# Attention units: order of decay exponentials and scores, place of the normalisation, and gate and finish steps on GpSimd

## What is computed

```python
qkvgr = einsum('btc,oc->bto', layernorm(x), W)         # q, k, v (16 heads of 8) and 16 gates
log_G = cumsum(log_sigmoid(gates), axis=time)          # per head
Z = 2*log(abs(q @ k.T) + 1e-7) + log(scale) + log_G[t] - log_G[s]     # causal
P = exp(Z - rowmax);  y = (P @ v) / sum(P);  x = x + y
```

## Time and profile before

| | |
|---|---|
| three executions | 1281.03, 1281.9, 1283.69 us, median 1281.9 |
| the profiled execution | 1283.27 us |
| its span, first to last instruction | 1281.4 us |
| attention, units of all batches | from 36 to 462 us of the span |
| busy in the span | PE 884.1, PEld 610.8, DVE 769.8, ACT 531.4, POOL 502.0 us |
| granted TensorE clock, mean | 0.816 of full |

### The profile page before, as it was taken

How to read it: one execution, slowest core, us unless ns; L and a number is a source line. 1 busy time by engine, 2 the same in 40 slices (tenths; PEclk the granted TensorE clock), 3 DMA queues, 4 the chain that set the end, 5 groups by cost and what they waited for, 6 DMA issues and landing times. The chain is left out here.

```text
span 1281.4 us, 25926 instructions
## 1 busy us (share of the span) xinstructions
PE 884.1 (69%) x9215; PEld 610.8 (48%) x9215; DVE 769.8 (60%) x1623; ACT 531.4 (41%) x1192; POOL 502.0 (39%) x545
## 2 busy tenths in 40 slices
PE   4778778786877834079937599947776783407993
PEld 2445354453644521068823278616565572106882
DVE  6576685766766674012254079999999999401223
ACT  4557465565646621034514430025555540104441
POOL 3452434534345321714430000027777770172442
PEclk9978696887968867579978889977888887758997
DMA  6133140322404041167732930000002100016775
GB/s 188 48 115 103 38 140 14 128 71 70 137 5 140 2 166 45 54 164 197 206 101 102 254 74 1 1 0 1 0 0 65 33 17 17 11 54 166 203 198 160
DMA packets 134915, 111.75 MB, mean 87 GB/s; under 512 B 27248, under 2 KB 120368, under 8 KB 134384
## 3 DMA queue, kind: packets, MB, share of 16 engines
q1 hardware_dynamic: 129264, 99.66, 26.3%
q0 software_dynamic: 5120, 10.53, 2.4%
q10 hardware_dynamic: 432, 0.20, 0.1%
HBM read 64.80 MB, written 45.43 MB: 86 GB/s over the span
## 5 line engine op out<-in xcount | busy, mean ns | idle before, releaser
L624 DVE TENSOR_SCALAR a_mag<-a_pS 128x1024 int32<-128x1024 int32 (+1 forms) x192 | 176.7, 949 | 90.6 <-PE a_pS L831 90.6
L406 ACT ACTIVATE a_pw<-a_mag,a_eps_a 128x1024 f32<-128x1024 f32 (+1 forms) x192 | 173.4, 930 | 98.0 <-DVE a_mag L624 93.3
L299 POOL TENSOR_TENSOR a_pw<-a_pw,a_decay 128x256 f32<-128x256 f32 x128 | 97.2, 763 | 244.8 <-ACT a_pw L406 244.7
L1125 POOL DMA_INDIRECT ys_dram<-f_yo,f_who x96 | 91.9, 958 | 129.4 <-DVE f_yo L1325 112.7
L1313 DVE TENSOR_SCALAR f_ysT<-f_bY,f_b2s 128x256 f32<-128x256 f32 x48 | 23.2, 483 | 175.8 <-PE f_bY L1413 173.2
L831 PE MATMUL a_pS<-a_qf,a_kf 64*64 64x192 bf16 (+3 forms) x1536 | 115.6, 278 | 14.8 <-DVE a_mag L624 13.1
L1672 POOL TENSOR_TENSOR d_pb_p<-d_Q,d_s_sb 128x512 f32<-128x512 f32 x32 | 37.3, 1166 | 196.4 <-ACT d_s_sb L1772 196.4
L1168 ACT ACTIVATE f_hs<-f_bH,f_b1s 128x256 f32<-128x256 f32 x192 | 75.4, 475 | 66.5 <-PE f_bH L1403 66.5
L2145 PE MATMUL d_c<-d_pb_p,d_ident 128*128 128x256 f32 x256 | 73.5, 457 | 41.8 <-POOL d_pb_p L1678 41.8
L1117 POOL DMA_INDIRECT xs_dram<-f_xa,f_pos x64 | 61.6, 962 | 93.9 <-DVE f_pos L1298 75.0
L1403 PE MATMUL f_bH<-f_xsT,f_w1s 128*128 128x256 f32 x384 | 95.2, 392 | 0.0
(11 more groups left out here) (342 smaller groups left out, 1777.6 us busy)
## 6 DMA issues: line engine op xcount, KB each, us to landing
parts_scratch<-a_parts SPq DMA_DIRECT2D x32, 384.0 KB, 3.3
f_w1s<-in_L_ffn_w_dram SPq DMA_DIRECT2D x48, 256.0 KB
f_w2s<-in_L_ffn_w_dram SPq DMA_DIRECT2D x48, 256.0 KB
a_kf<-parts_scratch SPq DMA_DIRECT2D x16, 512.0 KB, 5.1
a_qf<-parts_scratch SPq DMA_DIRECT2D x16, 512.0 KB, 6.2
xs_dram<-blank SPq DMA_DIRECT2D x12, 516.0 KB, 5.3
f_xs<-xs_dram SPq DMA_DIRECT2D x48, 129.0 KB, 2.3
parts_scratch<-a_parts SPq DMA_DIRECT2D x16, 256.0 KB, 3.0
```

The lines of the kernel that those rows point to most:

```text
L299: pool.tensor_tensor(own, own, decay[:, k, m, hf:NP:2, :], ALU.mult)\
L406: act.activation(pw[:, n % 4, 0:N], mag[:, n % 3, 0:N], ACT.Square, bias=eps_a[:, 0:1])\
L624: dve.tensor_scalar(mag[:, n % 3, 0:2 * N].bitcast(I32).rearrange("p (l t) -> p l t", l=2), pS[:, 2 * (n % 2):2 * (n % 2) + 2, 0:N].bitcas ...
L1125: pool.indirect_dma_start(ys_dram[f][:, :], bass.IndirectOffsetOnAxis(ap=who[:, q, a:a + 1], axis=0), yo[:, q, a, :], None).then_inc(ys_ou ...
```

## The change

- The steps TURN, QK and VALUES come one step earlier (4, 6, 9), and the second half's finish too (FIN 18, 2). The value copies on ScalarE so move from step 14 to 13, `gate_logs` stays at 13.
- ScalarE: `decays` come first in their step, ahead of off_copy and square.
- TensorE: `scores(n + 2)` come first in their step.
- VectorE: `normalize` moves from step 20 to TURN + 1 = 5. The steps on the gates (`gate_low`, which were the second half of `gate_prep`, and `gate_log`) leave it for all batches but the first, and so do product and addition of the finish (L654, L659) for all halves but the very last.
- GpSimd takes them: `add_half` for the second half at step 4 and for the first half at step 20, `gate_low` at step 12 (three instructions, where VectorE had two) and `gate_log` at step 14, each behind that step's diagonal; add_half and gate_low are ahead of that step's `values_off` and `split_low`. `split_low` stays at steps 10 and 11.

```diff
-        TURN, QK, VALUES, SUMS, DECAY = 5, 7, 10, 15, 22
-        FIN = (18, 3)
+        TURN, QK, VALUES, SUMS, DECAY = 4, 6, 9, 15, 22
+        FIN = (18, 2)
@@ gpsimd @@
+            def gate_low(bb):
+                pool.wait_ge(s["gate_sb"], 4 * bb + 3)
+                pool.wait_ge(s["logg_done"], bb)
+                pool.tensor_scalar(g_low[:, :], gates[:, :], 0.0, None, ALU.min).then_inc(s["gate_sb"], 1)
+                pool.wait_ge(s["gate_sb"], 4 * bb + 4)
+                step(pool.tensor_tensor(g_abs[:, :], g_low[:, :], gates[:, :], ALU.subtract))
+                pool.tensor_tensor(g_abs[:, :], g_abs[:, :], g_low[:, :], ALU.add).then_inc(s["g_step"], 1)
+            def gate_log(bb):
+                pool.wait_ge(s["g_step"], 3 * bb + 3)
+                pool.wait_ge(s["cum_ps"], bb)
+                pool.tensor_tensor(logg[:, :], g_low[:, :], g_abs[:, :], ALU.subtract).then_inc(s["logg_done"], 1)
+            def add_half(b, k, hf):
+                step = 5 * (2 * b + hf)
+                pool.wait_ge(s["fin_step"], step + 3)
+                pool.tensor_tensor(y[:, :, :, :], acc[:, :, :, 0:HD],
+                                   rnorm[:, :, :].unsqueeze(3).broadcast_to([P, 16, 2, HD]), ALU.mult)\
+                    .then_inc(s["fin_step"], 1)
+                pool.wait_ge(s["fin_step"], step + 4)
+                xs = x[:, TT * b:TT * b + TT, :].rearrange("p i (a c) -> p (i a) c", c=32)[:, :, 16 * hf:16 * hf + 16]
+                pool.tensor_tensor(xs, xs, y[:, :, :, :].rearrange("p a x d -> p a (x d)"), ALU.add)\
+                    .then_inc(s["fin_step"], 1)
...
+                    if n == FIN[1] + 2 and not first:
+                        add_half(b - 1, 1 - k, 1)
+                    if n == FIN[0] + 2:
+                        add_half(b, k, 0)
                     if last:
                         continue
-                    if QK + 3 <= n < QK + 5:
-                        split_low(b + 1, n - QK - 3)
+                    if n == VALUES + 3:
+                        gate_low(b + 1)
+                    if n == VALUES + 5:
+                        gate_log(b + 1)
+                    if QK + 4 <= n < QK + 6:
+                        split_low(b + 1, n - QK - 4)
@@ scalar: batch @@
                 for n in range(NU):
+                    if not first:
+                        for m in decay_pair(n + NU - DECAY - 1):
+                            decays(b, k, m)
+                    if not last:
+                        for m in decay_pair(n - DECAY - 1):
+                            decays(b + 1, 1 - k, m)
                     if n == 1 and not first:
                         off_copy(b - 1, 1)
                     if n == HU + 1:
                         off_copy(b, 0)
                     square(b, n)
...
-                    if n == VALUES + 3:
+                    if n == VALUES + 4:
                         gate_logs(b + 1)
@@ vector: batch @@
                     if n == FIN[0] + 1:
-                        for part in (2, 3, 4):
-                            finish(b, k, 0, part)
+                        finish(b, k, 0, 2)
                     if n == FIN[1] + 1 and not first:
-                        for part in (2, 3, 4):
-                            finish(b - 1, 1 - k, 1, part)
+                        finish(b - 1, 1 - k, 1, 2)
...
-                    if n == 20 and b + 2 < B:
+                    if n == TURN + 1 and b + 2 < B:
                         normalize(b + 2)
...
-                    if n == VALUES + 3:
-                        gate_log(b + 1)
@@ tensor: batch @@
                 for n in range(NU):
+                    if n + 2 < NU:
+                        scores(b, k, n + 2)
+                    elif not last:
+                        scores(b + 1, 1 - k, n + 2 - NU)
                     if n == FIN[1] and not first:
                         turn_back(b - 1, 1)
...
-                    if n + 2 < NU:
-                        scores(b, k, n + 2)
-                    elif not last:
-                        scores(b + 1, 1 - k, n + 2 - NU)
```

More of the change, by code:

```diff
@@ L422, in batch @@
                     square(b, n)
-                    if not first:
-                        for m in decay_pair(n + NU - DECAY - 1):
-                            decays(b, k, m)
                     if last:
                         continue
-                    for m in decay_pair(n - DECAY - 1):
-                        decays(b + 1, 1 - k, m)
                     if n == TURN + 1:
@@ L556, in gate_prep @@
                 dve.wait_ge(s["v_ps"], bb + 1)
+                if bb:
+                    dve.wait_ge(s["g_step"], 3 * bb - 2)
                 for q, M in enumerate((M0, M1)):
@@ L678, in _ @@
             gate_prep(0)
+            gate_low(0)
             rstds(1, B, 6)
```

## The result

| | median of runs, us | lowest to highest | ratio to before, 95% interval |
|---|---|---|---|
| before | 1282.29 | 1281.03 to 1283.69 | |
| after | 1271.55 | 1268.58 to 1273.27 | 0.9914, 0.9892 to 0.9935 |

What follows compares the result with a forecast made beforehand. No engine is full in the attention; TensorE, busiest (some 43 of a batch's 54 us), waits most for ScalarE's decay exponentials, 31.1 us. Terms: -31.1 + 0 + 9.8 + 0.7 = -20.6 us, forecast 1262 us, range 1245 to 1276.

Steps and rivals of the forecast that it cites:

- The two waits at the boundary: Between batches, decay sums wait 1.66 us (the first) and 2.33 us for ScalarE's exponentials; both go, gain 31.1 us.
- The gate chain: Steps 13 to 14: gate_log on GpSimd behind diagonal(14) starts gate sums 1.4 us later: +9.8 us, bounds 6 to 13.
- Steps 2 to 11: Normalisation moves in at 1.0 to 2.3 us, finish work of 0.85 leaves; taken as 0, bounds -3 to +9 us.
- The turn-back's 6.4 us: Steps 16 to 21: TensorE's wait for the turn-back, 6.4 us over the seven-boundary stretch, claimed to stay.
- The last batch: End of the attention: add_half at step 20 delays diagonal(21) by 1.5 us, VectorE gains: +0.7 us, bounds 0 to 1.5.
- The two rivals on GpSimd: Released waits return on GpSimd's queue, steps 20 to 23 (1272, 12%), or its lock with VectorE at step 5 (1274, 11%).
- the second rival: Step 5: normalisation blocked by GpSimd instructions takes 3.0 us instead of 1.0; +12 us, 1274 us, 11%.
- I follow TensorE from step 22 (about 192) with the clock as it was: At the boundary, TensorE's steps costed at 1.2 GHz as before: scores 1.0, two decay sums 2.1, attend 0.4 to 0.7 us.
- low time in steps 15 to 21 is harmless: Argument against the slower rival: VectorE sets the pace in steps 15 to 21, so low clock there costs nothing.
- the slower rival: Longer idle before the gate sums (2.9 us, not 1.45) holds the low clock through steps 2 to 14: 1295 us, 5%.
- The clock rival: Boundary: without its two idle times TensorE gets 2.4 GHz earlier, 17 us more gained: 1245 us, 17%.
- the prediction's own signs: Attention in the profile after: a mean clock clearly under 0.8 would make the forecast wrong.

Runs made afterwards that it cites:

- e1: The kernel before with only ScalarE's decays moved to the head of their step: 1238.5 us, ratio 0.9665.
- e2: The kernel before with only the normalisation moved from step 20 to step TURN + 1: 1263.1 us, ratio 0.9853.
- e3: The changed kernel with gate_log on GpSimd at step 13 instead of 14, ahead of diagonal(14): 1257.9 us, ratio 0.9786.
- e12: The changed kernel with gate_log on GpSimd at step 13 and scores back in their old place: 1252.5 us, ratio 0.9770.
- e8: The changed kernel with scores back in their old place in TensorE's step: 1264.7 us, ratio 0.9839.
- e6: e1 plus the normalisation moved to step TURN + 1: 1240.0 us, ratio 0.9636.
- e7: e1 plus product and addition of each half's finish on GpSimd (add_half): 1243.8 us, ratio 0.9681.
- e11: e1 with the value copies on ScalarE moved to step 13, ahead of square(14): 1241.5 us, ratio 0.9694.
- e9: e1 with scores first in TensorE's step only in steps 22, 23, 0 and 1: 1261.5 us, ratio 0.9846.
- e10: e1 with scores first in TensorE's step only in steps 2 to 21: 1252.3 us, ratio 0.9696.
- e4: The changed kernel with the value copies on ScalarE back behind square(14), at step 14: 1259.5 us, ratio 0.9739.

## Why the prediction was right in its range, and off by half in its gain

- **The two waits at the boundary** (-31.1): right in cause and size. L812's waits went from 31.1 us to none, and the boundary stretch (scores(22) to scores(4) of the next batch) from 22.5 to 18.2 us, 29.1 us less over the seven. Right also that the first wait belonged to normalisation and order together: e1 and e2 each remove it.
- **The gate chain** (+9.8): right. The waits grew by 9.6 us, at 2.84 a batch against the 2.9 forecast, and taking the chain away gives 13.7 back (e3). But the steps behind them grew by 13.6 us, see below. The size of gate_low was short: 0.53 and twice 0.46 us instead of 0.4 each; its slack hid that.
- **Steps 2 to 11** (0, bounds -3 to +9): +2.7 us in steps 2 to 14, inside. The normalisation's four instructions took 1.9 us, within the 1.0 to 2.3 allowed for. The turn-back's 6.4 us, said to stay, went; the waits of scores for magnitudes took 5 of them.
- **The last batch** (+0.7): +1.1 us, from its scores(4) to the end of the attention.
- **The two rivals on GpSimd** did not come in: attends wait for GpSimd 7.8 us against 7.2, and the normalisation's four instructions take 1.9 us where the second rival has 3.0.
- **The step that failed** is "I follow TensorE from step 22 (about 192) with the clock as it was", which the sum does everywhere, together with "low time in steps 15 to 21 is harmless". The sum treated busy time as fixed; it rose by 13.8 us (338.0 to 351.9), which is more than the whole distance between 20.6 forecast and 11.8 found in the attention. Most of the rise, 9.0 us, is in steps 15 to 19. These were at a clock of 1.00 in four of the seven batches before, and are at 0.75 to 0.87 in all seven after, behind the 2.84 us wait. They last 12.6 to 13.1 us where the clock is 0.86 or 0.87 and 13.6 where it is 0.75; before, at 1.00, they lasted 10.8, and the longer wait alone would add 1.4. So the stretch grew by 13.6 us and not by 9.8. This is the mechanism of the slower rival at a small size, in the steps where the prediction ruled it out. Without the long wait these steps are at 1.00 again in five (e3) and seven (e12) of the seven batches; but of the busy time of the whole attention only 2.6 us come back in e3, and 6.9 from e8 to e12. So the wait brings the low clock to these steps, and what holds the total up is open.
- **The sum again, by stretches**: -29.1 + 13.6 + 2.7 + 1.1 gives the 11.8 found, to 0.1. The boundary was forecast at its low clock and kept it, so the order "scores first", costed at nothing, took little from the forecast there (29.1 us gained for 31.1, with 1.4 us more of busy time). What it took is a gain that the forecast did not count on and that e1 has.
- **The clock rival** (1245 us, 17%) named the right possibility and the wrong kernel: a boundary without waits can run at 2.4 GHz. In the profiled executions of e1, e6 and e7 one boundary of seven does so throughout, and the busy time of e1's attention is 17.4 us below the kernel before; in the changed kernel none does.
- **The range and the signs.** The bounds of the terms, added up, give 1254 to 1282 us; the 1251 to 1274 of the text does not follow from them. Either takes the measured time in, and so does the stated range, whose upper end was set by the rivals on GpSimd. But what lies between forecast and result is mostly busy time, for which the sum had no term and no bound, so it is partly luck that the range holds. By the prediction's own signs, a mean clock clearly under 0.8 in the attention was to count against it, and it is 0.78.

The Trainium skill ("TensorE: Matmul & The Clock Gate", What's actually happening) says that activity releases the throttle and that the idle state is the slow one. The wait for the gate sums fits it. Of the seven batches, steps 15 to 19 are partly low in all seven behind a wait of 2.8 us (after, e8), in one to three behind one of 1.5 (three in the kernel before, one in e1), in two behind one of 0.5 (e3) and in none behind one of 0.4 (e11, e12). The boundary does not fit a plain reading of it: in e9 TensorE was busy for 17.4 of 19.0 us and stayed at the lower level for nearly all of it (0.55). Why the clock stays low there is not settled. Shown is that the order of scores and decay sums has a part in it (e9 against e1), and that it does not decide alone (e10, and the seven boundaries of e1). Whether it is the kind of matmul at a given moment or the moment at which TensorE reaches the boundary could not be told apart, since every order moves both.

## What to carry to other kernels

Where an in-order engine holds a result back behind work whose input comes later, moving the short instruction with the ready input to the head of the step was worth the whole wait here, and this one edit alone won more than the large change that it was part of (44.6 us against 10.7): measure the parts alone before they are joined. A busy time is no constant: cost each new order at both clock levels, and after each edit read TensorE's busy time over the same instructions beside its idle time. And an instruction that moves to another engine inherits that engine's queue: gate_log takes 0.46 us there instead of 0.28, but it costs 1.4 us of waiting a batch through standing behind diagonal(14), and through it behind square(14) and the value copies.

## What was not expected of the hardware

- The same 200 matmuls of a boundary took from 10.81 us of TensorE's busy time (clock 1.00) to 17.40 (0.55); within one execution of e1, with one order, from 10.81 to 17.24.
- Executions of one kernel can disagree by 20 us: e4 ran at 1240.9, 1258.8, 1260.2 and 1261.1 us, e10 at 1242.2, 1242.7, 1252.3, 1260.8 and 1261.0 us, where e9 stayed within 2.5 us.
- On GpSimd a tensor_scalar on 128x128 with one input took 534 ns by the profile, longer than a tensor_tensor with two, 458. On VectorE the former took 0.23 us before the change.
